# Attention layers of a graph kernel in three single-pass products, with the first product of all heads ahead of them

## What is computed

```python
def _gat_layer(x, src, dst, W, a_src, a_dst, bias, concat):
    H, C = a_src.shape                       # 4 heads x 512, then 1 head x 768
    h = (x @ W).reshape(N, H, C)
    al_s = jnp.einsum('nhc,hc->nh', h, a_src)
    al_d = jnp.einsum('nhc,hc->nh', h, a_dst)
    e = jax.nn.leaky_relu(al_s[src] + al_d[dst], 0.2)
    alpha = softmax of e over the edges into each dst
    out = segment_sum(h[src] * alpha, dst)
    return (concatenated heads, or mean) + bias
h   = jax.nn.elu(_gat_layer(x, src, dst, W1, att_src1, att_dst1, b1, concat=True))    # 1250 x 2048
out = _gat_layer(h, src, dst, W2, att_src2, att_dst2, b2, concat=False)               # 1250 x 768
```

## Time and profile before

| | before |
|---|---|
| runs | 3828.39, 3830.29, 3833.73 us |
| median | 3830.29 us |
| profiled execution | 3831.38 us, of which the span of the instructions is 3829.5 us |
| mean granted TensorE clock | 0.944 of full speed |
| busy share | TensorE 89%, weight loads 74%, VectorE 53%, ScalarE 32%, GpSimd 24% |

### The profile page before, as it was taken

How to read it: one execution, slowest core, us unless ns; L and a number is a source line. 1 busy time by engine, 2 the same in 40 slices (tenths; PEclk the granted TensorE clock), 3 DMA queues, 4 the chain that set the end, 5 groups by cost and what they waited for, 6 DMA issues and landing times. The chain is left out here.

```text
span 3829.5 us, 57503 instructions
## 1 busy us (share of the span) xinstructions
PE 3419.3 (89%) x19326; PEld 2819.8 (74%) x19326; DVE 2038.9 (53%) x3973; ACT 1230.5 (32%) x2195; POOL 905.5 (24%) x992
## 2 busy tenths in 40 slices
PE   4998898998989696999999898999998899599994
PEld 3885454544545365999999788999997767499994
DVE  4987433424333453111587761124878633799996
ACT  1243212212122111111344431113445400278883
POOL 1103755656300000000355530003545300000000
PEclk9988899998999798999999899999999989799997
DMA  2022001000000012334676653335766510100001
GB/s 75 25 64 64 17 1 42 1 25 17 9 16 0 20 34 103 98 98 136 212 239 215 209 172 120 99 101 199 238 216 211 164 56 21 66 1 0 0 0 41
DMA packets 120966, 328.22 MB, mean 86 GB/s; under 512 B 26144, under 2 KB 67661, under 8 KB 120802
## 3 DMA queue, kind: packets, MB, share of 16 engines
q0 software_dynamic: 55408, 208.93, 17.6%
q1 hardware_dynamic: 65394, 117.16, 8.9%
HBM read 243.20 MB, written 82.83 MB: 85 GB/s over the span
## 5 line engine op out<-in xcount | busy, mean ns | idle before, releaser
L585 PE MATMUL bank<-arena 125*125 (+3 forms) x3600 | 762.3, 368 | 0.0
L1430 PE MATMUL bank<-w_hi,xT_hi 128*125 128x384 f32 x1920 | 652.3, 340 | 17.0 <-ACT arena L1218 9.6
L585 PEld LDWEIGHTS bank<-arena 125*125 125x125 f32 x3600 | 497.6, 190 | 229.1 <-issue 176.8
L1431 PE MATMUL bank<-w_lo,xT_hi 128*125 128x384 f32 x1920 | 650.7, 339 | 0.0
L1432 PE MATMUL bank<-w_hi,xT_lo 128*125 128x384 f32 x1920 | 650.7, 339 | 0.0
L1218 ACT COPY arena<-bank 125x384 f32<-125x384 f32 x320 | 153.5, 480 | 807.9 <-PE bank L1432 717.3
L1430 PEld LDWEIGHTS bank<-w_hi,xT_hi 128*125 128x125 f32 x1920 | 358.3, 187 | 18.8 <-issue 12.2
L718 DVE SCALAR_TENSOR_TENSOR row_lo<-arena,edges,row_hi 128x768 fp32r<-128x768 f32 x300 | 304.3, 1014 | 119.4 <-ACT row_hi L685 78.5
L1431 PEld LDWEIGHTS bank<-w_lo,xT_hi 128*125 128x125 f32 x1920 | 358.1, 186 | 0.1
L1432 PEld LDWEIGHTS bank<-w_hi,xT_lo 128*125 128x125 f32 x1920 | 357.9, 186 | 0.1
L1799 DVE CAST w_hi<-w_raw 128x2304 fp32r<-128x2304 f32 x36 | 48.9, 1359 | 562.9 <-PE bank L1432 513.9
(11 more groups left out here) (308 smaller groups left out, 5033.6 us busy)
## 6 DMA issues: line engine op xcount, KB each, us to landing
y_early<-arena SPq DMA_DIRECT2D x200, 187.5 KB
w_raw<-in_L_gnn_W_dram POOLq DMA_DIRECT2D x32, 1152.0 KB
y_late<-arena SPq DMA_DIRECT2D x120, 187.5 KB
arena<-in_L_gnn_W_dram SPq DMA_DIRECT2D x8, 1536.0 KB, 6.8
wadj_d<-arena SPq DMA_DIRECT2D x10, 625.0 KB
arena<-wadj_d SPq DMA_DIRECT2D x1, 6250.0 KB
mask_d<-arena POOLq DMA_DIRECT2D x10, 610.4 KB, 7.5
arena<-mask_d SPq DMA_DIRECT2D x1, 6103.5 KB
```

Of the source, the lines that this page charges most:

```text
L585: ins = pe.matmul(bank[b][0:P, 0:w], tsc[:, t], f, start=(t == 0), stop=(t == NT - 1))
L1430: pe.matmul(b, xT_hi[:, k, v], w_hi[:, h, k], start=(k == 0), stop=False)
L1431: pe.matmul(b, xT_hi[:, k, v], w_lo[:, h, k], start=False, stop=False)
```

## The change

1. **First network in three products.** x W1, the sum of each unit, the product with W2 and the sums of the second layer take operands split into high and low parts, as the second network does: 3 instructions instead of 2. ScalarE writes the high parts and VectorE the low ones. Of x and W1, the first 500 nodes and head 0 are split at the end of the counting stage (`act_x_high(act, 0, k)`, `dve_x_low(dve, 0, k)`), ahead of VectorE's last work on the mask; the other 750 nodes come after `next_phase`.
2. **All of x W1 first.** 40 tiles (4 heads x 10) run in one stage. Each goes through a slot `h_stage` to `h_d` in DRAM, and two weighted sums of it are made on the way. Each head's features are loaded back as one transfer of 2.5 MB and split.
3. **Streamed mask.** Its place in SBUF goes to x and the features. GpSimd stores each finished mask tile in `own_mask_d` as well, and each unit loads its tile of 625 KB into one of two slots, once the unit two before it has used the slot.
4. **Overlapped heads.** The loops over heads are written out. The scores of the first two units of the next head are made during the last steps of this one, `s_row` comes from one transpose and ten small matmuls, and the logits of the second layer are summed in the last head.
5. **GCN.** `wadj`, `xs` and `agg1` are split and L1514 becomes three products. The splits stand beside the product before them.
6. **Index copies.** In the second network ScalarE makes the copies of L710, and GpSimd waits for VectorE's `tile_ready` besides.

The core of the diff:

```diff
+        def act_x_high(act, c, k):
+            act.copy(x0_hi[k][:, X_CUTS[c]], x0_raw[:, k, X_CUTS[c]]).then_inc(dense_high, 1)
+        def dve_x_low(dve, c, k):
+            dve.wait_ge(dense_high, c * KD + k + 1)
+            dve.tensor_tensor(x0_lo[k][:, X_CUTS[c]], x0_raw[:, k, X_CUTS[c]], x0_hi[k][:, X_CUTS[c]].bitcast(F32), op=ALU.subtract).then_inc(dense_low, 1)
...
+        def act_s_row(act, h, b0):
+            if h:
+                act.wait_ge(score_masked, unit(h * NT - 1))
+            for c in range(3):
+                ins = act_spread(act, h * NT, c, b0, s_row, s_row_low)
+            ins.then_inc(s_row_ready, 1)
...
+        def act_take_high(act, u):
+            act.wait_ge(agg_made, unit(u - 2))
+            for c, (t0, nt) in enumerate(PARTS):
+                act.wait_ge(score_turned, piece(u, c))
+                act.copy(tsc_hi[:, u % 2, t0:t0 + nt], bank[c][0:P, 0:nt * P].rearrange("p (t n) -> p t n", n=P)).then_inc(score_high, 1)
+        def dve_take_low(dve, u):
+            for c, (t0, nt) in enumerate(PARTS):
+                dve.wait_ge(score_high, 3 * u + c + 1)
+                dve.tensor_tensor(tsc_lo[:, u % 2, t0:t0 + nt], bank[c][0:P, 0:nt * P].rearrange("p (t n) -> p t n", n=P),
+                                  tsc_hi[:, u % 2, t0:t0 + nt].bitcast(F32), op=ALU.subtract).then_inc(turned_taken, 1)
...
+        def pe_sum(pe, u, banks, high, low_part):
+            for c, (t0, nt) in enumerate(PARTS):
+                pe.wait_ge(turned_taken, piece(u, c))
+                for t in range(t0, t0 + nt):
+                    if u % NT == 0:
+                        if u < H0 * NT:
+                            pe.wait_ge(feature_low, u + t + 1)
+                        else:
+                            pe.wait_ge(dense_low, 2 * KD + t + 1)
+                    for b, hi, lo in zip(banks, high(t), low_part(t)):
+                        w = hi.shape[-1]
+                        for i, (x, y) in enumerate(((tsc_hi, hi), (tsc_hi, lo), (tsc_lo, hi))):
+                            ins = pe.matmul(bank[b][0:P, 0:w], x[:, u % 2, t], y, start=(t == 0 and i == 0), stop=(t == NT - 1 and i == 2))
+            ins.then_inc(agg_made, 1)
...
+        def pe_part(pe, u):
+            h = u // NT
+            pe.wait_ge(hT_ready, unit(u))
+            pe.wait_ge(part_taken, unit(u - 1))
+            for k in range(KC0):
+                if u % NT == 0:
+                    pe.wait_ge(weight_low, H0 * KD + h * KC0 + k + 1)
+                for g in range(2):
+                    v = slice(g * HD, (g + 1) * HD)
+                    for i, (x, y) in enumerate(((hT_hi, w2_hi), (hT_hi, w2_lo), (hT_lo, w2_hi))):
+                        ins = pe.matmul(bank[6 + g][0:P, 0:HD], x[:, k], y[h % 2][:, k, v], start=(k == 0 and i == 0), stop=(k == KC0 - 1 and i == 2))
+            ins.then_inc(part_made, 1)
...
+        def dve_hidden_low(dve, u):
+            dve.wait_ge(hT_high, u + 1)
+            dve.tensor_tensor(hT_lo.rearrange("p k n -> p (k n)"), bank[5][:, 0:KC0 * P], hT_hi.rearrange("p k n -> p (k n)").bitcast(F32),
+                              op=ALU.subtract).then_inc(hT_ready, 1)
...
+            done = runs[NT] + HB if c else 0
             def body(j, y):
                 for k in range(GT):
                     pool.wait_ge(idx_ready, (j + past) * GT + (k + 1))
+                    pool.wait_ge(tile_ready, (j + done) * GT + ((HB - 1) * GT + k + 1))
...
+                    next_index(act, k, order_idx[:, bass.ds(place_of(j, k) + GT, 1), IDX_AT])
...
-                next_index(dve, k, order_idx[:, bass.ds(at + GT, 1), IDX_AT])
...
+            def load_mask(u):
+                if u >= 2:
+                    sp.wait_ge(score_masked, unit(u - 2))
+                sp.dma_start(mask_slot[:, u % 2], own_mask_d[u % NT * P:(u % NT + 1) * P, :]).then_inc(mask_in[u % 2], 16)
...
+            for q in range(H0 * NT):
+                h, n = divmod(q, NT)
+                sp.wait_ge(h_ready, q + 1)
+                sp.dma_start(h_d[h][n * P:(n + 1) * P, :], h_stage[:, q % 4]).then_inc(h_stored[q % 4], 16)
...
+                for e in range(max(d - 1, 0), NT if d == NT - 1 else d):
+                    pool.wait_ge(own_ready, e + 1)
+                    pool.dma_start(own_mask_d[e * P:(e + 1) * P, :], mask[:, e]).then_inc(own_stored[0 if e < 7 else 1], 16)
...
+            act.wait_ge(own_stored[0], 16 * 7)
+            for k in range(KD):
+                act_x_high(act, 0, k)
+                act_w1_high(act, 0, k)
             act_sqrt(act, "sqrt_act", dinv_win[:])
             next_phase(act)
-            with act.Fori(0, H0) as h:
-                for n in range(NT):
-                    act.wait_ge(h_made, unit(h * NT + n))
-                    if n == 0:
-                        act.wait_ge(agg_made, unit(h * NT - 1))
-                    act.copy(h_head[:, n], bank[5 + n % 2][0:P, 0:C0]).then_inc(h_ready, 1)
-                act.wait_ge(acc_cleared, 1)
-                act_s_row(act, h, s_row)
-                act_units(act, h, score, turned_score, True)
+            for k in range(KD):
+                act_x_high(act, 1, k)
+            act.wait_ge(own_stored[1], 16 * (NT - 7))
...
+            for h in range(H0):
+                more = h + 1 < H0
+                for s in range(NT + 1):
+                    u = h * NT + s
+                    if s < NT and (s or not h):
+                        act_take_high(act, u)
+                    if s >= 2:
+                        act_hidden_high(act, u - 2)
+                    if s + 2 < NT:
+                        act_unit_exp(act, u + 2, u + 2, score[:, u % 2])
+                    if more and s == 2:
+                        act_row_turn(act, h + 1, bank[2][0:NT, 256:256 + P])
+                    if more and 5 <= s < 5 + KC0:
+                        act_w2_high(act, h + 1, s - 5)
+                    if more and s == NT:
+                        act_s_row(act, h + 1, 0)
+                        act_unit_exp(act, u, u, score[:, 0])
+                        for t in range(2):
+                            act_h_high(act, h + 1, t)
+                        act_unit_exp(act, u + 1, u + 1, score[:, 1])
+                    if s:
+                        act_elu(act, u - 1)
...
+                    if h == 0 and n in (0, 4):
+                        pe.wait_ge(dense_low, KD * (n // 4) + k + 1)
+                    if n == 0:
+                        pe.wait_ge(weight_low, h * KD + k + 1)
+                    v = slice(n * P, (n + 1) * P)
+                    for i, (x, w) in enumerate(((x0_hi, w1_hi), (x0_hi, w1_lo), (x0_lo, w1_hi))):
+                        ins = pe.matmul(bank[q % 4][0:P, 0:C0], x[k][:, v], w[h % 2][:, k], start=(k == 0 and i == 0), stop=(k == KD - 1 and i == 2))
+                ins.then_inc(h_made, 1)
...
+            pe.wait_ge(h_ready, H0 * NT)
+            for h in range(H0):
+                more = h + 1 < H0
+                for s in range(NT + 2):
+                    u = h * NT + s
+                    if more and s == 3:
+                        pe.wait_ge(al_ready, h + 2)
+                    if s < NT and (s or not h):
+                        pe_unit_turn(pe, u, score[:, s % 2])
+                    if s >= 2:
+                        pe_hidden_turn(pe, u - 2)
+                    if more and s == NT:
+                        pe.wait_ge(turned_taken, piece(u - 1, 2))
+                        pe_s_row(pe, h + 1, 0)
+                    if 1 <= s <= NT:
+                        pe.wait_ge(hidden_ready, unit(u - 3))
+                        if u == 1:
+                            pe.wait_ge(s_row_ready, 1)
+                        pe_sum(pe, u - 1, [3 + (u - 1) % 2], lambda t: [h_hi[t]], lambda t: [h_lo[h % 2][t]])
+                    if more and s == 2:
+                        pe.wait_ge(al_done, (h + 2) * NT)
+                        pe.wait_ge(turned_taken, piece(u, 2))
+                        pe_row_turn(pe, h + 1, bank[2][0:NT, 256:256 + P])
+                    if more and s == NT + 1:
+                        pe.wait_ge(s_row_ready, h + 2)
+                        pe_unit_turn(pe, u - 1, score[:, 0])
+                    if s >= 2:
+                        pe_part(pe, u - 2)
...
+            for h in range(H0):
+                more = h + 1 < H0
+                for s in range(NT + 1):
+                    u = h * NT + s
+                    if s >= 3:
+                        dve_part(dve, u - 3)
+                        if not more:
+                            wide_logits(s - 3)
+                    if s >= 2:
+                        dve_hidden_low(dve, u - 2)
+                    if s < NT and (s or not h):
+                        dve_take_low(dve, u)
+                    if s + 2 < NT:
+                        dve_mask(dve, chain, u + 2)
+                    if more and 5 <= s < 5 + KC0:
+                        dve_w2_low(dve, h + 1, s - 5)
+                    if more and s == NT:
```

(38 more changed lines are left out.)

604 lines of the change are left out of this document (402 added, 202 removed).

## The result

The changed kernel took 3710.7 us, the median of four runs (3705.44 to 3717.0), against 3832.0 for the kernel before beside it: a ratio of 0.968 (95% interval 0.967 to 0.970), some 121 us less. I had forecast 3631, 199 less, in a range of 3575 to 3700. The sign was right, the size was not: the time lies 11 us above the range. The profiled execution spans 3703.8 us.

The account below looks back on a forecast made before the run. The prediction took TensorE to bound the heads. First network -210, second network -5 and GCN +16 sum to -199; 3831.4 - 199 = 3632, and with the median 1.1 below the profiled execution 3631, range 3575 to 3700.

Parts of the forecast that it names:

- Start of the heads: Between the last x W1 product and the first sum: 24 us for mask load, scores, exponential and transposes; first sum at 553.
- A unit: One unit of a head: TensorE needs 12.35 us where it was 16.20, with VectorE hidden by 0.4 to 1.2 us.
- Between heads: Head transitions: 2.5 us of stalls, 8 at unit 0, 3 at half clock, 3 for small matmuls; 140 us a head.
- the rival: Mask tile loads in the heads: stream too slow, each of 36 steps 5.5 us more, losing the 200 us; chance 0.02.
- Second layer: First network's second layer: first sum at 1137, sums and transposes 115 us plus 6 cold start; stage ends 1285 against 1495.8.
- The new price: Three split products replacing two float32 instructions on TensorE: 0.216 us for 512 columns, 0.175 for 384 and for 256.
- The floor: Split products on TensorE: at full clock each waits for its weight load, 0.175 us, and only wider ones exceed it.
- the other, with 0.20: Split products on TensorE: a fixed extra of 15 ns each, 0.228, 0.175 and 0.122 us; total 3622, chance 0.20.
- The product stage: All x W1 tiles: TensorE starts at about 345, waits for low parts (24 us) until 390, ends at 529.
- Second network: Gathers of the second network: index copies leave VectorE, mostly hidden, with an added wait on `tile_ready`; -5 us.
- the rival with the copies as bound: Second network: index copies bound the gathers, saving 25 us instead of 5; total about 3610, chance 0.10.
- VectorE as the bound of the units: Units of the heads: VectorE's chain exceeds the step, period 13.8 us, 54 us more; total 3685, chance 0.15.

Follow-up runs that it names:

- experiment 1: Against the changed kernel, SyncE sends the next head's features in five pieces and W2 in four, each behind a later mask tile; ratio 0.969 (0.967 to 0.971).

## Why the prediction was wrong

By its own steps:

- **"Start of the heads", "A unit", "Between heads".** The mask stream was priced only in the rival, as a rate: half of (load + 3.2), with the words that one or two loads may come near. The step that failed is that I did not put SyncE's queue in order of issue. One tile behind 4 MB in a queue that moves 124 GB/s is late by 21 us whatever the mean rate. I also took 1536 KB in 6.8 us from the earlier trace rows as the speed of all loads (230 GB/s); feature and mask transfers move at a little over half of that. The forecast had nothing for it; mask tiles ahead of the bulk gave 44 us back, and then head 1 takes 141.3 us and head 2 142.3 where I had said 140. That is luck in part: the sums of a head cost 5 us more than I had, by the price below, so the transitions between heads cost 2 to 4 less than my 16.5.
- **"Second layer".** The cycle of 12.7 us rested on a load of 3.1 us. It takes 9.5 to 11 with the rows of x ahead. Its price is 24 us (sums from first to last 140.1, forecast 122); the step was mis-sized, its mechanism right. "GpSimd's sort is done before half of the second layer" failed too: SyncE still waited 15.7 us for it there. Hidden in the changed kernel behind `leave_b`, it is what ended the gain of experiment 1.
- **"The new price".** The floor was wrong; of the two readings the other, with 0.20, was nearer, though most of the extra grows with the columns. 1920 instructions on 512 columns cost 0.016 more each, 30 us: 11 in the product stage, 19 in the sums (period 12.7 or more, not 12.35, when nothing is waited for). The dense sum costs 71 us instead of 105, so the GCN network came out 33 below. The Trainium skill's N/2.4 + 2.5 ns ("TensorE: Matmul & The Clock Gate", section "Back-to-back issue gap") gives 0.216 us for 512 columns and, as an estimate, 65 us for the dense sum; the rows, with 0.232 and 71, don't agree with it, nor does the 0.175 for 384 columns. The 30 us too little and the 34 too much nearly cancel in the total, by luck: the term was wrong at both widths.
- **"The product stage".** The low parts took 21.88 us against my 24, TensorE's waits for them 22.7: right. The first four tiles were done at 364.5, where I had 365, though 345 and four times 3.89 make 361; the 3.89 is for full clock, and from 345 to 371 the granted clock was 0.83. The phase boundary came at 371 instead of 366; GpSimd issued its last store of a mask tile at 361.4, and ScalarE's wait of 9.5 us for the boundary ended with GpSimd's queue. With the price above that makes the stage end at 545.6, forecast 529. The first sum was 33 us later instead of 24, as the first mask tile, issued at 547.04, landed only at 561, 12.7 us of VectorE's idle time.
- **The last attention.** I costed it at nothing, since its text is unchanged. It cost 23 us in the profiled execution and 20 to 51 in the other kernels with the stalls. No view of the kernel before could have told it: its loop has no idle time at the turns.
- **"Second network".** -5 forecast, -8 measured (-14.5 to the mean of twelve executions, all against one trace of before): right in kind, and the rival with the copies as bound is refuted.
- **The rivals.** VectorE as the bound of the units (0.15) did not happen: in mid-head the units come 12.7 to 13.1 us apart, with TensorE busy 49.79 of 50 us (640 to 690). The range missed since no case held two or three costs at once: mask tiles 44, second layer 24, last attention 23.

## What to carry to other kernels

Where a change streams what was resident, write out the queue in its order of issue: a tile is late by what stands ahead of it, waits of the issuing engine included, not by the mean rate. Issue what is needed next ahead of what is large, and put a wait on a slow helper last. Before taking "that stage is untouched" as zero, look at its loops: a program that grows can move them, and a stall of 2.5 us can cost two to four times that (23 to 38 us for four of them in two executions of the changed kernel) when TensorE's clock falls behind it.

## What the runs showed of the hardware

- A product of float32r operands takes 0.444 ns per column and about 5 ns at the high clock (0.118, 0.175 and 0.232 us for 256, 384 and 512 columns; a pass of a float32 matmul on 512 took 0.214); at the low clock 384 columns took 0.319, 0.83 ns per column with no extra.
- VectorE's loop over the same instructions (some 290 a turn in the trace) ran without a pause at two places in the program and lost 2.3 to 3.2 us at each of four turns at three others, with 27 packets of 8 KB on the instruction queue q14 in the stage against 7. Why those two places and not the others wasn't tried.
- VectorE's low parts from two SBUF inputs took 0.87 us with GpSimd waiting and 3.65 beside its elementwise work.
- Loads of mask tiles and features, on 125 partitions, moved at 124 to 134 GB/s with the transfer engines 33% busy, a 1536 KB weight on 128 partitions at 231 with 97%.
